# Slots of a routed expert layer: tokens found by one-hot products on chip in place of scatters and a gather

## The reference, cut to what matters

```python
hn2 = layernorm(x, ln2_g, ln2_b)            # 2048 tokens x 256
logits = hn2 @ gate_w + gate_b              # 2048 x 8
# every token goes through the expert of its largest logit:
x = x + relu(hn2 @ w1[e] + b1[e]) @ w2[e] + b2[e]
```

## Time and profile before

| | |
|---|---|
| median of 3 runs | 926.01 us (925.89 to 927.42) |
| the profiled execution | 924.24 us, span of its trace 922.5 us |
| busy, of the span | PE 715.2 us (78%), DVE 528.3 (57%), ACT 344.3 (37%), POOL 240.2 (26%) |
| second layer ends, experts begin | last output projection from 399.55 us, first expert product at 439.10 us |
| chain that ended last | PE 48%, DVE 24%, DMA 8%, issue 6%, ACT 6% |

### The profile page before, as it was taken

One profiled execution on the slowest core, in us unless ns is written; L12 is line 12 of the kernel. 1 busy time (PEld: TensorE's weight loads), 2 busy tenths in 40 slices (PEclk: granted clock), 3 DMA queues, 4 the chain that ended last, 5 costly groups with the idle time before them and its releaser, 6 DMA issues.

```text
span 922.5 us, 15737 instructions
## 1 busy us (share of the span) xinstructions
PE 715.2 (78%) x5815; PEld 539.4 (58%) x5815; DVE 528.3 (57%) x1283; ACT 344.3 (37%) x627; POOL 240.2 (26%) x234
## 2 busy tenths in 40 slices
PE   2657888878988888730999999964677769896898
PEld 2444656555655654420898899953544546575775
DVE  3547577887888786341112222224658888564585
ACT  1324454445546544500323222203044444543323
POOL 1513243333343322222102211005334441212000
PEclk9769898999999998855999999997598888865999
DMA  4969355865466573337556486503845432071002
GB/s 152 122 81 195 60 100 75 118 95 80 76 136 71 84 161 116 128 115 149 176 178 199 140 237 172 166 26 59 102 80 78 85 68 48 14 292 60 36 3 90
DMA packets 59848, 101.94 MB, mean 111 GB/s; under 512 B 7715, under 2 KB 50147, under 8 KB 54613
## 3 DMA queue, kind: packets, MB, share of 16 engines
q1 hardware_dynamic: 57357, 95.75, 47.5%
q0 software_dynamic: 2416, 5.19, 2.8%
HBM read 55.30 MB, written 7.28 MB: 68 GB/s over the span
## 4 chain that ended last, share of the span: by engine, by line
PE 48%; DVE 24%; DMA 8%; issue 6%; ACT 6%; SPq 4%; POOL 4%; ACTq 0%; DVEq 0%; POOLq 0%
PE PS L792 8%; PE U L803 8%; PE MB L635 7%; PE MB L730 4%; DVE nma L1152 4%; PE U L708 4%; PE PS L690 3%; DVE R L1356 3%; SPq L1566 2%; PE MB L667 2%; DMA La<-Uba 2%; DMA QKa<-mTa 2%; PE MB L882 2%; PE PS L847 2%; PE MB L651 1%
## 5 line engine op out<-in xcount | busy, mean ns | idle before, releaser
L1152 DVE TENSOR_REDUCE nma<-MB 128x2 f32<-128x512 f32 (+1 forms) x192 | 123.1, 670 | 32.7 <-PE MB L667 32.2
L970 ACT ACTIVATE Pa<-PS 128x1024 f32<-128x1024 f32 (+1 forms) x96 | 97.9, 1024 | 59.2 <-PE PS L690 57.9
L667 PE MATMUL MB<-QKa 99*128 99x120 bf16 (+1 forms) x512 | 73.6, 258 | 30.8 <-DVE nma L1152 15.8
L792 PE MATMUL PS<-mzT,mw 128*128 128x128 f32 x736 | 87.5, 278 | 1.8 <-ACT mzT L992 1.8
L803 PE MATMUL U<-mw,mdT 128*128 x368 | 83.5, 380 | 4.8 <-ACT mdT L1002 2.4
L792 PEld LDWEIGHTS PS<-mzT,mw 128*128 128x128 f32 x736 | 85.4, 194 | 2.7 <-issue 2.3
L1312 DVE TENSOR_TENSOR yt<-U,mb 128x256 f32<-128x256 f32 x23 | 9.8, 425 | 120.9 <-PE U L803 120.9
L667 PEld LDWEIGHTS MB<-QKa 99*128 99x128 bf16 x512 | 38.9, 104 | 64.2 <-DVE nma L1152 28.8
L803 PEld LDWEIGHTS U<-mw,mdT 128*128 128x128 f32 x368 | 68.2, 190 | 13.8 <-issue 5.5
L1400 POOL TENSOR_TENSOR mv<-mv,vec 128x2 f32<-128x2 f32 (+1 forms) x40 | 31.1, 777 | 140.5 <-DVE mv L1103 93.3
L690 PE MATMUL PS<-QKa 101*128 101x256 bf16 (+1 forms) x384 | 61.6, 285 | 3.1 <-DMA QKa<-mTa 3.1
(11 more groups left out here) (198 smaller groups left out, 1356.8 us busy)
## 6 DMA issues: line engine op xcount, KB each, us to landing
mw<-in_mw SPq DMA_DIRECT2D x31, 1024.0 KB, 6.0
QKa<-spa SPq DMA_DIRECT2D x144, 128.0 KB, 5.0
Qb<-spb SPq DMA_DIRECT2D x48, 128.0 KB, 4.4
Oa<-Uba SPq DMA_DIRECT2D x16, 256.0 KB, 3.6
v<-in_v SPq DMA_DIRECT2D x1, 4096.0 KB, 13.8
v<-in_v SPq DMA_DIRECT2D x4, 1024.0 KB, 11.9
W<-in_W SPq DMA_DIRECT2D x3, 1280.0 KB, 6.7
yb<-yt SPq DMA_DIRECT2D x23, 128.0 KB, 1.7
```

The source lines that it names most:

```text
L667: i = e.matmul(b[:, keys * j:keys * j + keys], Q[0:99, h0 + j, 128 * qt:128 * qt + 128], K[0:99, h0 + j, 0:keys], start=True, stop=True)
L792: i = e.matmul(ps[:, 128 * f:128 * f + 128], w[:, k, 128 * f:128 * f + 128], zz[:, k, :], start=k == 0, stop=k == 1)
L970: e.activation(p[0:keys, :], ps[0:keys, :], ACT.Exp, scale=0.25).then_inc(sems["exp"], 1)
L1152: e.tensor_reduce(A.nm[qt][:, h0:h0 + heads], b[:, 0:heads * keys].rearrange("p (h s) -> p h s", h=heads), AX.X, ALU.max, negate=True).the ...
```

## The change

- The scatters (16), the table `ib` in DRAM with its zero fill, the gather `ids` and its transpose are gone.
- For each batch VectorE splits `posf` into the number of its 128-slot block (`tile`) and the slot in it (`row`): one addition of 1.5 x 2^30 rounds to a multiple of 128. It then writes, for both token tiles, two one-hot rows of 128: `tile_of` (which block) and `row_of` (which slot, times the token number). `gs` becomes a TensorE step: the product of the two, summed over the two token tiles, is a 128 x 128 table of token numbers, which VectorE adds to `slot_ids`. Its place moves from 2.7 to 2.85.
- In `cnt` VectorE makes `place_of`, a one-hot matrix from the 128 blocks to the 23 tiles, and TensorE multiplies `slot_ids` by it; the cast to `rows_of` follows. `te` is now finished after `rows_of`. `bex` moves into `own`.
- A new constant `rowc` (287 columns) is loaded at time 9.8, in the space of the first layer's weights, once these are used up.
- The third layer's weights, which go to that same space, are loaded in tile 1, behind tile 3's `w1`, once `rows_of` is made.
- The last two `w2` loads wait until the last attention output has landed. The second tile's `w1` waits for the first gathered rows, formerly for `ids`.

```diff
-T_AFTER = (1.75, 2.0, 2.2, 2.35, 2.6, 2.7)
+T_AFTER = (1.75, 2.0, 2.2, 2.35, 2.6, 2.85)
-T_LOADS = (-3.2, -1.5, -0.5, 0.5, 1.0, 1.6)
+T_LOADS = (-3.2, -1.5, -0.5, 0.5, 1.0)
-        ((NB + 2.5,), [[("w3",)]]),
+        ((NB + 1.8,), [[("rc",)]]),
...
+        elif what == "gs":
+            yield s, ("slots", key[0] - 7)
...
     # TensorE
+        def slot_table(n):
+            b, k = bank("gs", n), n % 2
+            g.wait_ge("marks", 4 * (n - 7))
+            g.free(BANKS.free["gs", n])
+            for t in range(2):
+                i = e.matmul(b[:, 0:128], tile_of[k][:, t, :], row_of[k][:, t, :], start=t == 0, stop=t == 1)
+            i.then_inc(sems["slot_mm"], 1)
         def table():
-            g.wait_ge("d_i", 16)
+            g.wait_ge("slots", 8)
+            g.wait_ge("cnt", 6)
-            e.transpose(b[:, 0:128], ids[:, :], idf[:, :]).then_inc(sems["table"], 1)
+            e.matmul(b[:, 0:NTILE], slot_ids[:, :], place_of[:, :], start=True, stop=True).then_inc(sems["table"], 1)
...
     # VectorE, end of gate_rank
-            e.tensor_copy(pos[:, two(b)], posf[:, two(b)]).then_inc(sems["rank"], 1)
+            e.tensor_scalar(u, posf[:, two(b)], -63.75, ROUND, ALU.add, ALU.add).then_inc(sems["rank"], 1)
+            g.wait_ge("rank", k + 5)
+            g.wait_ge("marks", 4 * b)
+            e.tensor_scalar(tile, u, ROUND, None, ALU.subtract).then_inc(sems["rank"], 1)
+            g.wait_ge("rank", k + 6)
+            e.tensor_tensor(row, posf[:, two(b)], tile, ALU.subtract).then_inc(sems["rank"], 1)
+            g.wait_ge("slot_mm", b - 1)
+            for t in range(2):
+                e.tensor_scalar(tile_of[n % 2][:, t, :], rowc[:, R_TILE:R_TILE + 128], tile[:, t:t + 1], None, ALU.is_equal
+                                ).then_inc(sems["marks"], 1)
+            g.wait_ge("rank", k + 7)
+            for t in range(2):
+                c = C_TOK + 2 * b + t
+                e.tensor_scalar(row_of[n % 2][:, t, :], rowc[:, R_ROW:R_ROW + 128], row[:, t:t + 1], cst[:, c:c + 1],
+                                ALU.is_equal, ALU.mult).then_inc(sems["marks"], 1)
+        def add_slots(n):
+            b, m = n - 8, bank("gs", n)[:, 0:128]
+            g.wait_ge("slot_mm", b + 1)
+            if b == 0:
+                e.tensor_copy(slot_ids[:, :], m).then_inc(sems["slots"], 1)
+            else:
+                g.wait_ge("slots", b)
+                e.tensor_tensor(slot_ids[:, :], slot_ids[:, :], m, ALU.add).then_inc(sems["slots"], 1)
...
     # VectorE, table(): cnt, cmp, nt as before, then
+            add_slots(15)
+            e.tensor_tensor(below[:, :], nt[:, :], rowc[:, R_BELOW:R_BELOW + 8], ALU.mult).then_inc(sems["cnt"], 1)
+            e.tensor_reduce(spot[:, :], below[:, :], AX.X, ALU.add).then_inc(sems["cnt"], 1)
+            e.tensor_scalar(place_of[:, :], rowc[:, R_PLACE:R_PLACE + NTILE], spot[:, 0:1], None, ALU.is_equal
+                            ).then_inc(sems["cnt"], 1)
...
...
     # POOL: scatter(), table() and the memset are gone
-                e.indirect_dma_start(ib, slots(t), cst[:, C_TOK + t:C_TOK + t + 1], None).then_inc(sems["d_s"], 16)
...
     # SyncE
+            if k == 6:
+                g.wait_ge("d_o1", 16 * 8)
...
             tile_weights(0)
-            g.wait_ge("d_i", 16)
+            g.wait_ge("d_z0", 16)
             tile_weights(1)
...
+            if j == 1:
+                g.wait_ge("rows_of", 1)
+                load_weights(2)
```

More of the change, by code:

```diff
@@ L143, in order @@
     out += pipeline(0, 16, [
-        (T_LOADS, [[("ld", i)] for i in range(6)]),
-        ((NB + 2.5,), [[("w3",)]]),
+        (T_LOADS, [[("ld", i)] for i in range(5)]),
+        ((NB + 1.8,), [[("rc",)]]),
         (T_WEIGHTS, [[("ew", k)] for k in range(7)])])
@@ L496, in build @@
     yt = ma.ring("yt", 3, [128, 256])
+    sa = Area(s_at - 20480, s_at - 10240)
+    rowc = sa.new("rowc", [128, 287])
+    tile_of = sa.ring("tile_of", 2, [128, 2, 128])
+    row_of = sa.ring("row_of", 2, [128, 2, 128])
+    slot_ids = sa.new("slot_ids", [128, 128])
+    place_of = sa.new("place_of", [128, NTILE])
+    below = sa.new("below", [128, 8])
+    spot = sa.new("spot", [128, 1])
+    split_pos = sa.new("split_pos", [128, 3, 2])
     fa, ta = Area(s_at - 10240, s_at), Area(s_at - 20480, s_at - 10240)
@@ L1253, in table @@
             e.tensor_tensor(tej[:, :, :], over(binc[:, :], NTILE, 1), over(cst[:, C_J:C_J + NTILE], 8, 2),
                             ALU.is_le).then_inc(sems["cnt"], 1)
-            g.wait_ge("cnt", 7)
+            g.wait_ge("cnt", 9)
             e.tensor_reduce(tef[:, :], tej[:, :, :], AX.X, ALU.add).then_inc(sems["cnt"], 1)
[L1257 to L1278, removed]
             g.wait_ge("table", 1)
             e.tensor_copy(rows_of[:, :], bank("cnt")[:, 0:NTILE]).then_inc(sems["rows_of"], 1)
+            g.wait_ge("cnt", 10)
+            e.tensor_scalar(tef[:, :], tef[:, :], 7.0, None, ALU.min).then_inc(sems["cnt"], 1)
@@ L1282, in own_rows @@
+            g.wait_ge("cnt", 11)
+            e.tensor_copy(te[:, :], tef[:, :]).then_inc(sems["cnt"], 1)
         def own_rows():
+            e.tensor_tensor(bex[:, :], binc[:, :], nt[:, :], ALU.subtract).then_inc(sems["own"], 1)
+            g.wait_ge("own", 1)
             e.tensor_scalar(offs[:, :], bex[:, :], 128.0, None, ALU.mult).then_inc(sems["own"], 1)
[L1284 removed]
+            g.wait_ge("own", 2)
             e.tensor_tensor(offs[:, :], offs[:, :], cst[:, C_BASE:C_BASE + 8], ALU.subtract).then_inc(sems["own"], 1)
[L1286 removed]
+            g.wait_ge("own", 3)
@@ L1386, in constants @@
                 e.memset(o[:, 2, :], 0.0).then_inc(sems["ohb0"], 1)
-        def loads(i):
-            if i == 5:
-                e.memset(y[:, 0, 0:128], 0.0).then_inc(sems["y0"], 1)
         def norm_stats(n, i):
@@ L1427, in add_y @@
             e.tensor_tensor(x[:, two(b), :], x[:, two(b), :], y[:, two(b), :], ALU.add).then_inc(sems["xy"], 1)
-        def scatter(n):
-            b = n - 8
-            g.wait_ge("d_zero", 16)
-            g.wait_ge("d_cst", 16)
-            g.wait_ge("rank", 5 * (b + 1))
-            for t in (2 * b, 2 * b + 1):
-                e.indirect_dma_start(ib, slots(t), cst[:, C_TOK + t:C_TOK + t + 1], None).then_inc(sems["d_s"], 16)
-        def table():
-            g.wait_ge("d_s", 256)
-            g.wait_ge("cnt", 20)
-            e.indirect_dma_start(ids[:, :], None, ibv, bass.IndirectOffsetOnAxis(ap=coli[:, 0:1].bitcast(U32), axis=0)
-                                 ).then_inc(sems["d_i"], 16)
         def fetch(j):
@@ L1477, in clear @@
                 e.memset(b[:, :, :, :], 0.0).then_inc(sems["bd0"], 1)
-        does = {"in": constants, "ld": loads, "na": norm_stats, "qp": lambda n: split_rest("qp", n),
+        does = {"in": constants, "na": norm_stats, "qp": lambda n: split_rest("qp", n),
                 "kp": lambda n: split_rest("kp", n), "qs": lambda n: split_low("qp", n), "ks": lambda n: split_low("kp", n),
-                "of": offset, "xy": add_y, "gs": scatter, "cnt": table, "fe": fetch, "ro": tile_in, "bg": gather_back,
+                "of": offset, "xy": add_y, "fe": fetch, "ro": tile_in, "bg": gather_back,
                 "ft": front_turn, "fw": front_choice, "ex": clear}
```

79 lines of the change are left out of this document (39 added, 40 removed).

## The result

The changed kernel takes 909.26 us (median of 4 runs, 908.86 to 911.76) against 925.95 us before (4 runs, 923.51 to 927.42). The ratio is 0.9828, 95% interval 0.98 to 0.9856: 16 to 17 us faster, where I had forecast 11. In a second set of runs (after_again) it took 913.49 us against 927.53, ratio 0.9856 (0.9826 to 0.9886). All ratios here compare fast runs alone; one run of b_late (2262.0 us) and one of b_warm (1397.25 us) were slow and are left out of them. The profiled execution took 908.86 us with a span of 906.4, 16.1 us less than the span of before.

A forecast was written before the change was run, and what follows sets the result against it. TensorE starved between the second attention layer and the experts (404.0 to 439.1 us); earlier no engine alone was the bound. Terms: -13.0 passage, -1.5 last sums, -2.5 stalled transfer, +6.5 batches = -10.5 us; forecast 915.0, range 907 to 921.

The forecast's parts named there:

- the passage: From the second attention layer to the experts: without the table's DMAs the first expert product starts 13.0 us sooner.
- rival A: First expert weights still take 11.3 us, as a first touch would; start only 7.7 us sooner, 920 us; chance 0.12.
- The batches: Batches 8 to 14: splits, marks and addition cost VectorE net 1.7 us each, charged as 6.5 us, bounds 0 and 12.
- The stalled transfer: The 7.03 us transfer at 280.33, behind scatters, falls to its like; 2.5 us gained, bounds 0 and 3.5.
- The last sums: End of the second attention layer: holding the last two w2 loads lets these sums land sooner, 1.5 us gained.
- B: Rival: additions fit VectorE's idle time and scatters disturbed more; batches cost 2, stall gives 3.5; 909 us; chance 0.2.
- C (crowding): Rival: the third layer's weights and b2 push one expert's load late by their 4 us; 919 us; chance 0.1.
- signs of being wrong: Batch period over 2 us longer in 250 to 350 us, TensorE idle before slot products, or expert product released by weight load.
- part 2: Start of the experts: later-queued weight loads, the third layer's included, stay hidden behind work; cost 0.
- the 34 to 38 that I gave: Sign of being right: 34 to 38 us from the last sums' issue to the first expert product, where it was 48.4.
- D: Rival: TensorE stands before slot products waiting for marks; at 3 us a batch 930 us, slower than before; chance 0.05.

The follow-up runs named there:

- b_late: The kernel before with one number changed, the place of the scatter step gs, 2.85 for 2.7; 951.80 us, ratio 1.0244.
- b_warm: The kernel before with spare TensorE products, read by nobody, in its waits before the experts, 110 of them in the wait for the table; 926.48 us, ratio 0.9988.
- scat_last: The changed kernel with the scatters of batch 15 alone put back, their table read by nobody; 919.53 us, ratio 0.9891.
- no_wait: The changed kernel with the last two w2 loads issued at once, as before the change; 911.47 us, ratio 0.9785.
- no_marks: The changed kernel without the split, marks, products and additions of batches 8 to 14, other slots gathering row 0; 911.96 us, ratio 0.9820.
- b_few: The kernel before without the scatters of batches 8 to 14, so most slots gather row 0; 924.48 us, ratio 0.9955.
- POOL's marks: The changed kernel with the four marks of batches 8 to 14 made by POOL instead of VectorE; 912.61 us, ratio 0.9817.
- scat_all: The changed kernel with the scatters of all eight batches put back, their table read by nobody; 948.07 us, ratio 1.0204.

## Why the prediction was right, and where it was not

The time, 909.26, lies in the range, but the parts are less right than the sum. Of the spans' 16.1 us, the passage gave 14.1 (forecast 13.0) and the second layer 5.1 (forecast 2.5 us longer), and what follows the first expert product took 3.0 back (forecast 0). That two misses had opposite signs is luck.

**The passage (-13.0 forecast, 14.1 measured, with tile 0's slower start 13.0).** The steps came nearly as worked out. rows_of ended 4.9 us behind the end of posf where I had 4.8. Two small misses cancelled there: the slot products did not hide (1.24 us where I had 0.75, VectorE idle 0.59 for them), and the marks and the counting were shorter by 0.2. te came behind it and w1 was issued 1.1 us later. The load was what was late next, and took 4.9 where I had 5.7. The inference that its 11.3 us came from the scatter is shown by scat_last (11.45) against no_wait (4.96); rival A falls. Its argument that only this load was so slow was also wrong: the third tile's, issued at 431.58 behind two others in its queue, took 11.86 us before and 12.41 after. What I left out is that a first tile which starts sooner also starts while TensorE is at its low clock: 6.26 us, 1.1 more. The Trainium skill ("DMA: Bandwidth & Descriptors", Queues, rings and completion order) says that a DMA's semaphore increment lands only after every earlier write of the same engine, across its queues. That fits a load held by a scatter, but it says nothing of the rate: b_late shows the flow itself down to a fifth (61 against 333 GB/s).

**The batches (+6.5 forecast).** This term was mis-sized. The marks and the rest are 1.6 us of VectorE a batch as forecast (u to the end of row_of 1.5, the addition 0.29, less the cast; I had 1.7). But they cost 0.65 to 0.86 and not 1.36 in a full batch, and 2.4 to 3.5 us in all (no_marks). By itself a mark takes 0.28 us (`tile_of`) or 0.34 (`row_of`), and the four together 0.92, 0.23 each, where I had 0.25. The estimate of 0.13 from the Trainium skill ("VectorE: DVE Perf Modes", the perf-mode tier table) was too low by more; the measured time decides.

**The stalled transfer (-2.5 forecast).** Far too small. Removing seven pairs of scatters is worth 6.4 us in the layer (b_few), where this term and the next had 4.0 together. With the cheaper marks it made the gain 16 in place of 11. I had looked for one transfer on the chain; the scatters held others too. Without them the six sums transfers are used 0.2 to 2.2 us sooner each (b_few against before), in the batches 12 to 15 too, which have little VectorE work.

**The last sums (-1.5 forecast for the held w2 loads).** Right that they would land sooner, wrong in the cause. no_wait shows no cost of issuing the loads at once. Of the forecast's steps this is the one that failed as stated; what made them quicker belongs to the scatters of batch 13.

Together for the layer: -6.4 from the scatters and +3.5 for the marks leave -2.9. The two traces of the changed kernel show -5.1 and -2.0; the sum of the parts lies between them, and the two traces differ mostly by the clock's low stretches (18.1 and 24.6 us of low clock over the layer).

**Rivals and signs.** B came closest, and its 909 is the measured time: the marks cost less than I charged (2.4 to 3.5, B had 2) and the scatters disturbed more (6.4, B had 5.0 with the last sums). That the figure fits so well is luck, since B too had nothing for what is lost behind the first product. C (crowding) came to 0.8 of its 4 us: the third layer's weights landed in 11.1 us and tile 3 and 4 followed at the usual 7.25 us, but a later tile stood until its weights landed (482.08). That is a product released by a weight load, one of my signs of being wrong, and part 2's cost of 0 was not quite right. The 3.0 us lost behind the first product are tile 0's 1.1, that 0.8, and 1.4 behind the last row gather, less 0.4 that one tile of the kernel before had waited. From the last sums' issue to the first product it took 32.0 us, less than the 34 to 38 that I gave. D did not come: TensorE did not stand before the slot products of full batches. Open are what sets the places of the low-clock stretches, where the 1.4 us come from, and why POOL's marks gained nothing.

## What to carry to other kernels

A scatter of a few bytes a row is not only as long as its own landing: look in the trace at what the transfers around it take, and at the distance of issue between it and the next small transfer on the chain, since small transfers issued up to 3 us behind a scatter took 6.7 to 12.8 us here (b_late, scat_all) and those 5 to 8 us behind at most 7.1 (the kernel before). Finding positions by one-hot products costs about 1.6 us of VectorE and 0.6 of TensorE per 256 tokens, of which the chain saw about half where VectorE was full. And where the chain runs through f32 products of a starved TensorE, spare products in its waits can halve their time; where the chain is DMA they give nothing.

## What the runs showed of the hardware that was not expected

- Behind two indirect scatters of 128 elements of 4 bytes the flow on the DMA queues was 61 GB/s for 8.2 us where it was 333 (b_late, the changed kernel) and 38 for 8.4 us where it was 268 (scat_last, no_wait), and a 16 KB transfer took up to 12.84 us.
- Gathers of 128 rows most of which are the same DRAM row are slower than those of different rows: median 5.8 us against 4.4, and the loads of w1 beside them 7.0 us against 5.7 (b_few against before).
- Stretches of 3.4 or 6.8 us at a granted clock of 0.50 come at other places, or longer or shorter, from one execution of a kernel to the next (18.1 and 24.6 us over the second layer in the two traces of the changed kernel); 3.4 us more went with a batch 1.1 to 1.9 us longer in four of five places.
